# Self attention's key product by seven products of 2x2 blocks in place of eight, with both halves' scores behind the seventh product

## The chip, the cores and the metric

The kernel runs on one core of one Trainium2 chip, in one launch. The metric is device time in microseconds (us). A core has a matrix engine (TensorE, PE in the profile), a vector engine (VectorE, DVE), a scalar engine (ScalarE, ACT), GpSimd (POOL) and SyncE (SP), which here only issues DMAs. Each takes its instructions in the order written; an instruction may first wait until a semaphore has reached a count.

## The reference, cut to what matters

A decoder layer on 8 sequences of 100 tokens with 512 features, a context of 722 rows for each, and a second feed-forward part whose output is scaled by a gate. All is fp32.

```python
x0 = layernorm(x)                                   # (8, 100, 512)
q = x0 @ in_proj_w[:512].T + in_proj_b[:512]
k = x0 @ in_proj_w[512:1024].T + in_proj_b[512:1024]   # <- the product that is changed
v = x0 @ in_proj_w[1024:].T + in_proj_b[1024:]
sa = softmax(q @ k.T / sqrt(512)) @ v @ out_proj_w.T + out_proj_b
y = layernorm(x0 + sa) * g1 + be1
y = layernorm(y + cross_attention(y, ctx)) * g2 + be2
y = layernorm(y + relu(y @ w1.T + b1) @ w2.T + b2) * g3 + be3
x = x + y
out = x + gate_weight(x1 @ Wg) * (relu(x1 @ ffn_w1) @ ffn_w2)   # x1 = layernorm(x)
```

## The kernel before, in words

**Tiling.** The 800 tokens are two halves h of 400 columns (4 sequences each). Features lie on the partitions, as 4 chunks k of 128. A weight product ("unit" n, half h) of a 512x512 matrix makes 4 groups e of 128 output features, each in one PSUM bank: 4 chunks times 3 matmuls of 128x400. Three, since each fp32 operand is split into a high part (rounded to fp32r by ACT, names ending in H) and a low part (the rest, by a subtraction on DVE or POOL, ending in L): high times high, high times low, low times high. So a unit's half is 48 matmuls (lines 808 to 810).

**Self attention.** U_Q makes qT, U_K makes kT, U_VO is the output projection already multiplied by the value weights (`combine_high`, `combine_low` at the start). S_CQ and S_CK are the query and key weights of cross attention, which are multiplied together later (`combine_cross`). The order on PE (lines 1122 to 1144):

```python
unit(U_Q, 0); unit(U_K, 0, [0]); to_features(0, 1, tiles[1]); unit(U_K, 0, [1, 2, 3])
unit(U_Q, 1); self_scores(0); unit(U_K, 1); self_prob_transpose(0); combine_bias()
self_scores(1); self_attend(0); unit(U_VO, 0, [0, 1, 2]); self_prob_transpose(1)
unit(U_VO, 0, [3]); self_attend(1); to_tokens(1, 0, U_VO, XS); unit(U_VO, 1, [0, 1, 2])
```

`self_scores(h)` multiplies qT and kT of a half. DVE takes the maximum (`self_max`), ACT the exponential (`self_exp`), DVE the reciprocal (`self_normalise`), ACT scales (`self_normalise`), PE transposes (`self_prob_transpose`), ACT copies to sprobT (`self_probT`), and PE multiplies by the tokens (`self_attend`). ACT and DVE split the result into QH and QL (`self_attended`), the operand of U_VO. `self_attend(1)` writes bank k only when DVE has taken group k of U_VO's first half out of it (line 1011).

**Where splits and loads stand.** ACT splits the weights of a later unit between the groups of an earlier one (`SPLIT_AT`, line 1270): S_CQ in unit (U_K, 1), S_CK in unit (U_VO, 0), two chunks behind group 0, one behind group 1, one behind group 2. ACT's `self_probT(1)` comes behind group 2's. The low parts of S_CQ and S_CK are POOL's. DVE makes three sums of weights by a bias vector (`bias_product`: u_o, u_q, u_k); u_q reads the raw S_CQ weights in WR, u_k the raw S_CK weights in WR.

**SP's queue.** All loads are in one queue, in order: the context ct(0), the weights S_CQ, cn(0), ct(1), the weights S_CK, U_CV, and so on. ct(1) goes where ct(0) lay, so its two halves wait for DVE's `split_ct(0, 0)` and `split_ct(0, 1)` (line 558). S_CK goes to WR, so it waits for S_CQ's low parts and for u_q (lines 546 and 548). It stands behind ct(1).

**Products of 2x2 blocks.** `strassen(n)` (line 820) is already used for five feed-forward units: the 512x512 weights and the 512x800 operand are cut in 2x2 blocks, POOL makes four sums of weight blocks and four of operand blocks, ACT and DVE split them, PE makes 7 products of 12 matmuls in place of 8 (84 matmuls for both halves in place of 96), and DVE adds them up.

## Time and profile before

| what | value |
|---|---|
| time, median of 3 runs | 511.75 us (511.29 to 511.86) |
| the profiled execution's own time | 512.02 us |
| its span, first to last instruction | 510.1 us |
| PE busy | 503.7 us, 99% of the span, 2958 matmuls |
| DVE busy | 374.3 us, 73% |
| ACT busy | 242.7 us, 48% |
| POOL busy | 137.5 us, 27% |
| granted TensorE clock, mean | 1.000 |

Busy is the time in which an engine works on an instruction; waits for semaphores are not in it. PE's busy time counts pipelined matmuls, so it says that PE is never left waiting, not that each matmul takes the time shown for it: the distance from one start to the next does. The chain that ended last is followed back from the end of the program, at each step to what released the instruction.

### The profile page before, as it was taken

Reading aid. Unit: us, or ns where it says so; the run is one execution under the profiler, and the core shown is the slowest. Engines: PE = TensorE matmul, PEld = TensorE weight load, DVE = VectorE, ACT = ScalarE, POOL = GpSimd, SP = SyncE. Lnnn points to the kernel's source line nnn. Section 1 sums busy time; section 2 is a strip of 40 time slices with the busy share of each in tenths; the row PEclk is TensorE's granted clock in tenths of the full one; section 3 lists DMA queues with packets and bytes.
Section 4 is the critical chain, followed back from the end, with each engine's and each line's share of the span. In section 5 each row is a group of like instructions: output and inputs, shape, how many; then the busy total and the mean of one; then the engine's idle time right before and its main releaser. Section 6 shows DMA issues by size and latency. Waiting matters only on the chain.

```text
span 510.1 us, 7640 instructions
## 1 busy us (share of the span) xinstructions
PE 503.7 (99%) x2958; PEld 485.2 (95%) x2958; DVE 374.3 (73%) x644; ACT 242.7 (48%) x429; POOL 137.5 (27%) x104
## 2 busy tenths in 40 slices
PE   8999999999999999999999999999999999999997
PEld 6899999899988888999999999999999899999996
DVE  4853769786799896787699777368586878796645
ACT  3853652465598876164644334206536632442210
POOL 2430541014023134154504000444438313030000
PEclk9999999999999999999999999999999999999999
DMA  8951122031689961213521242002202022202004
GB/s 222 349 206 59 60 84 82 1 116 59 225 287 325 318 219 49 82 25 123 125 82 66 89 159 84 1 1 75 91 2 82 2 84 82 84 0 84 2 0 130
DMA packets 18508, 53.76 MB, mean 105 GB/s; under 512 B 1704, under 2 KB 2504, under 8 KB 15912
## 3 DMA queue, kind: packets, MB, share of 16 engines
q1 hardware_dynamic: 18412, 53.21, 31.5%
q8 instruction: 24, 0.39, 0.3%
q10 hardware_dynamic: 60, 0.07, 0.1%
q14 instruction: 12, 0.10, 0.1%
HBM read 51.63 MB, written 1.64 MB: 104 GB/s over the span
## 4 chain that ended last, share of the span: by engine, by line
PE 97%; DMA 1%; SPq 1%; DVE 0%; issue 0%; ACT 0%; DVEq 0%
PE ps L808 18%; PE ps L810 18%; PE ps L809 18%; PE ps L872 5%; PE ps L871 5%; PE ps L870 5%; PE ps L926 3%; PE ps L900 2%; PE ps L1067 2%; PE ps L1068 2%; PE ps L1069 2%; PE ps L1041 2%; PE ps L1043 2%; PE ps L1042 2%; DMA OR<-wvo_in 1%; PE ps L1013 1%
## 5 line engine op out<-in xcount | busy, mean ns | idle before, releaser
L808 PE MATMUL ps<-AH,WH 128*128 128x400 f32 x284 | 98.5, 347 | 0.0
L810 PE MATMUL ps<-AH,WL 128*128 128x400 f32 x284 | 98.0, 345 | 0.0
L809 PE MATMUL ps<-AL,WH 128*128 128x400 f32 x284 | 97.9, 345 | 0.0
L808 PE MATMUL ps<-XH,WH 128*128 128x400 f32 x192 | 66.7, 347 | 0.0
L810 PE MATMUL ps<-XH,WL 128*128 128x400 f32 x192 | 66.3, 345 | 0.0
L809 PE MATMUL ps<-XL,WH 128*128 128x400 f32 x192 | 66.2, 345 | 0.0
L651 POOL TENSOR_TENSOR WL<-WR,WH 128x512 fp32r<-128x512 f32 x29 | 41.4, 1457 | 69.8 <-ACT WH L1233 69.8
L808 PEld LDWEIGHTS ps<-AH,WH 128*128 128x128 f32 x284 | 53.4, 188 | 0.2
L809 PEld LDWEIGHTS ps<-AL,WH 128*128 128x128 f32 x284 | 53.4, 188 | 0.0
L810 PEld LDWEIGHTS ps<-AH,WL 128*128 128x128 f32 x284 | 53.4, 188 | 0.0
L1233 ACT ACTIVATE WH<-WR 128x512 fp32r<-128x512 f32 x60 | 34.1, 624 | 25.5 <-DMA WR<-wts_in 25.5
L1312 ACT ACTIVATE AH<-AT 128x400 fp32r<-128x400 f32 x40 | 21.2, 538 | 49.5 <-DVE AT L1660 32.6
L1622 DVE TENSOR_TENSOR acc<-ps,acc 128x400 f32<-128x400 f32 x47 | 26.5, 569 | 17.8 <-PE ps L810 17.6
L1579 DVE TENSOR_TENSOR ctL<-ctR,ctH 128x1444 fp32r<-128x1444 f32 x16 | 27.6, 1726 | 13.4 <-ACT ctH L1241 13.2
L808 PEld LDWEIGHTS ps<-XH,WH 128*128 128x128 f32 x192 | 36.1, 188 | 0.4 <-issue 0.2
L809 PEld LDWEIGHTS ps<-XL,WH 128*128 128x128 f32 x192 | 36.1, 188 | 0.1
L810 PEld LDWEIGHTS ps<-XH,WL 128*128 128x128 f32 x192 | 36.1, 188 | 0.0
L656 POOL TENSOR_TENSOR cnL<-cnR,cnH 128x1024 fp32r<-128x1024 f32 x7 | 16.9, 2411 | 53.4 <-ACT cnH L1247 53.4
L1665 DVE SCALAR_TENSOR_TENSOR AL<-AT,AH 128x400 fp32r<-128x400 f32 x40 | 28.1, 721 | 1.6
L1263 ACT ACTIVATE AT<-ps,cst 128x400 f32<-128x400 f32 x16 | 9.5, 595 | 40.7 <-PE ps L810 40.7
L645 POOL TENSOR_TENSOR rstd<-veps,nhalf 100x4 f32<-100x4 f32 x10 | 13.5, 1349 | 51.3 <-DVE veps L1747 51.2
L1574 DVE TENSOR_TENSOR WL<-WR,WH 128x512 fp32r<-128x512 f32 x28 | 18.2, 684 | 10.0 <-ACT WH L1233 10.0
(245 smaller groups left out, 1195.6 us busy)
## 6 DMA issues: line engine op xcount, KB each, us to landing
WR<-wts_in SPq DMA_DIRECT2D x19, 1024.0 KB, 4.8
ctR<-ctxt_in SPq DMA_DIRECT2D x16, 722.0 KB, 6.7
cnR<-ctxn_in SPq DMA_DIRECT2D x16, 512.0 KB, 4.9
cnR<-ctxn_in SPq DMA_DIRECT2D x8, 256.0 KB
tok<-x_in SPq DMA_DIRECT2D x8, 192.0 KB, 8.6
tok<-x_in SPq DMA_DIRECT2D x1, 1536.0 KB
cnR<-ctxn_in SPq DMA_DIRECT2D x8, 160.0 KB
VR<-wvo_in SPq DMA_DIRECT2D x4, 256.0 KB, 6.4
```

Source lines behind the costliest of these rows:

```text
L651: pool.tensor_tensor(WL[SLOT[n]][:, k, :], WR[:, k, :], raw(WH[SLOT[n]][:, k, :]), ALU.subtract).then_inc(w_low_pool, 1)
L808: pe.matmul(dst, wh, half(mh, h, k), start=(k == 0), stop=False)
L809: pe.matmul(dst, wh, half(ml, h, k), start=False, stop=False)
L810: mm = pe.matmul(dst, wl, half(mh, h, k), start=False, stop=(k == KC - 1))
L870: pe.matmul(dst, ah[:, k, cols], bh[:, k, :], start=(k == 0), stop=False)
L871: pe.matmul(dst, ah[:, k, cols], bl[:, k, :], start=False, stop=False)
L872: mm = pe.matmul(dst, al[:, k, cols], bh[:, k, :], start=False, stop=(k == 1))
L1233: act.activation(WH[SLOT[n]][:, k, :], raw_weights[:, k, :], ACT.Copy).then_inc(w_high, 1)
L1312: act.activation(half(AH, h, e), half(AT, h, e), ACT.Relu).then_inc(act_evac, 1)
L1579: dve.tensor_tensor(ctL[b % 2][:, 2 * i:2 * i + 2, 0:M], raw_ct(b, i), raw(ctH[b % 2][:, 2 * i:2 * i + 2, 0:M]), ALU.subtract).then_inc(ct ...
L1622: dve.tensor_tensor(half(acc, h, e), src, half(acc, h, e), ALU.add).then_inc(dve_evac, 1)
L1665: dve.scalar_tensor_tensor(out=half(AL, h, e), in0=half(AT, h, e), scalar=0.0, in1=raw(half(AH, h, e)), op0=ALU.max, op1=ALU.subtract).the ...
```

## The change

U_K is made by seven products of 2x2 blocks. The first two stand where unit (U_K, 0) stood; the other five follow unit (U_Q, 1). Both `self_scores` follow the seventh product, then `combine_bias`, then `self_prob_transpose(0)`. The raw key weights' sums are POOL's; the operand's sums t1 and t2 are DVE's, t3 and t4 POOL's. DVE adds the products up (`key_add`), in place of ACT's four evacuations for each half. ACT's splits of S_CQ, which stood in unit (U_K, 1), now stand between `self_normalise(0)` and `self_probT(0)`; DVE's `split_ct(0, 0)` and `split_ct(0, 1)` move behind u_q, whose last two steps move behind `self_normalise(1)`. cn(0)'s load waits for all of kT. The diff, cut:

```diff
-WHOLE = [n for n in LOADED if n not in STRASSEN]
+WHOLE = [n for n in LOADED if n not in STRASSEN and n != U_K]
...
             def load_cn(b, pieces=range(3)):
                 if b == 0:
-                    wait_w_low(sp, U_K, KC // 2 - 1)
-                    wait_w_low(sp, U_K, KC - 1)
+                    sp.wait_ge(k_out, 8)
...
             split_weights(U_Q, range(KC // 2))
-            for k in range(KC // 2, KC):
-                pool.wait_ge(w_high, KC * WHOLE.index(U_K) + k + 1)
-                pool.tensor_tensor(WL[SLOT[U_K]][:, k, :], WRK[:, k, :], raw(WH[SLOT[U_K]][:, k, :]),
-                                   ALU.subtract).then_inc(wk_low_pool, 1)
+            pool.wait_ge(wk_loaded, 16)
+            pool.tensor_tensor(s1, a21, a22, ALU.add).then_inc(k_sum, 1)
+            pool.wait_ge(k_sum, 1)
+            pool.tensor_tensor(s2, s1, a11, ALU.subtract).then_inc(k_sum, 1)
             inverse_deviation(1, 1)
-            pool.wait_ge(vo_made, KC)
+            pool.wait_ge(k_sum, 2)
+            pool.tensor_tensor(s4, a12, s2, ALU.subtract).then_inc(k_sum, 1)
+            pool.tensor_tensor(s3, a11, a21, ALU.subtract).then_inc(k_sum, 1)
+            pool.wait_ge(x_ready, KC)
+            for i in range(2):
+                ks = slice(2 * i, 2 * i + 2)
+                pool.tensor_tensor(X0[:, ks, :], raw(XH[0][:, ks, :]), raw(XL[0][:, ks, :]), ALU.add).then_inc(k_x0, 1)
+            pool.wait_ge(k_tsum, 2)
+            pool.wait_ge(k_x0, 2)
+            pool.tensor_tensor(t3, t2, X0[:, 0:2, :], ALU.subtract).then_inc(k_tsum_pool, 1)
+            pool.tensor_tensor(t4, t2, X0[:, 2:4, :], ALU.subtract).then_inc(k_tsum_pool, 1)
+            pool.wait_ge(s_scores, 1)
...
+            def key_products(products):
+                moving = [b(0, 0), b(0, 2)] + [key_sums(t) for t in range(4)] + [b(1, 2)]
+                for i in products:
+                    block_of = [0, 1, 3, 4, 2, 5, 6][i]
...
+                    for e in range(2):
+                        if e == 0:
+                            pe.wait_ge(k_low, block_of + 1)
+                            if 2 <= i < 6:
+                                pe.wait_ge(k_tlow, [1, 3, 4, 2][i - 2])
+                        if i < 2:
+                            pe.wait_ge(act_evac, act_count(U_Q, 0, 2 * i + e))
+                        elif i < 4:
+                            pe.wait_ge(k_tsum, 2)
+                        elif i < 6:
+                            pe.wait_ge(act_evac, act_count(U_Q, 1, 2 * (i - 4) + e))
+                        else:
+                            pe.wait_ge(k_three, e + 1)
...
             def self_scores(h):
-                pe.wait_ge(act_evac, act_count(U_K, h, KC - 1))
-                pe.wait_ge(x_ready, 2 * KC)
+                pe.wait_ge(act_evac, act_count(U_Q, h, KC - 1))
+                pe.wait_ge(k_out, 4 * (h + 1))
+                pe.wait_ge(k_two, 2)
...
             unit(U_Q, 0)
-            unit(U_K, 0, [0])
+            key_products([0])
             to_features(0, 1, tiles[1])
-            unit(U_K, 0, [1, 2, 3])
+            key_products([1])
             unit(U_Q, 1)
+            key_products(range(2, 7))
             self_scores(0)
-            unit(U_K, 1)
+            self_scores(1)
+            combine_bias()
             self_prob_transpose(0)
-            combine_bias()
-            self_scores(1)
             self_attend(0)
...
+            split_key(0)
+            split_key(1)
+            split_key(2)
             unit(U_Q, 0, [0, 1, 2])
             normalise(0, 1, tiles[1])
             unit(U_Q, 0, [3])
-            unit(U_K, 0, [0])
+            split_key(3)
+            act.wait_ge(k_sum, 4)
+            act.wait_ge(k_low, 3)
+            for e in range(2):
+                act.wait_ge(gemm_done, key_done(0, e))
+                act.activation(kmid[:, e, :], ps[:, KEY_BANKS[0] + e, 0:HALF], ACT.Copy).then_inc(k_first, 1)
             norm_features(0, 1)
-            unit(U_K, 0, [1, 2, 3])
+            for i in (4, 5, 6):
+                split_key(i)
+            split_key_sum(0)
+            unit(U_Q, 1, [0])
+            split_key_sum(3)
+            unit(U_Q, 1, [1])
+            split_key_sum(1)
+            split_key_sum(2)
+            unit(U_Q, 1, [2, 3])
+            self_exp(0)
             split_ct(0, 0)
-            unit(U_Q, 1)
-            self_exp(0)
-            split_ct(0, 1)
-            unit(U_K, 1, [0])
             self_normalise(0)
-            unit(U_K, 1, [1, 2, 3])
+            for k in range(KC):
+                split_weights(S_CQ, k)
             self_probT(0)
             self_exp(1)
             self_attended(0)
             self_normalise(1)
+            split_ct(0, 1)
             unit(U_VO, 0, [0, 1, 2])
             self_probT(1)
...
+            split_key(0)
+            split_key(1)
+            split_key(2)
             normalise(0, 1, tiles[1])
+            split_key(3)
             norm_features(0, 1)
+            dve.wait_ge(k_x0, 1)
+            dve.wait_ge(k_sum, 4)
+            dve.tensor_tensor(t1, ps[:, 4:6, 0:HALF], X0[:, 0:2, :], ALU.subtract).then_inc(k_tsum, 1)
+            dve.wait_ge(k_tsum, 1)
+            dve.tensor_tensor(t2, ps[:, 6:8, 0:HALF], t1, ALU.subtract).then_inc(k_tsum, 1)
+            for e in range(2):
+                key_add(1, e, half(kT, 0, e), kmid[:, e, :], k_out, col=e)
+            for i in (4, 5, 6):
+                split_key(i)
+            split_key_sum(0, 1); split_key_sum(3, 2); split_key_sum(1, 3); split_key_sum(2, 4)
...
-            unit(U_K, 0)
-            split_ct(0, 0)
-            unit(U_Q, 1)
-            bias_product(u_o, OR, C_BV, None, u_o_ready)
+            for e in range(2):
+                key_add(2, e, kmid[:, e, :], kmid[:, e, :], k_two)
+            for e in range(2):
+                key_add(3, e, half(kT, 1, 2 + e), kmid[:, e, :], k_three)
+            for e in range(2):
+                key_add(4, e, half(kT, 0, 2 + e), half(kT, 1, 2 + e), k_out, ALU.subtract, 2 + e)
+            bias_product(u_o, OR, C_BV, None, u_o_ready, [0, 1])
+            for e in range(2):
+                key_add(5, e, kmid[:, e, :], kmid[:, e, :], k_four)
+                key_add(5, e, half(kT, 1, 2 + e), half(kT, 1, 2 + e), k_out, col=2 + e)
+            bias_product(u_o, OR, C_BV, None, u_o_ready, [2, 3])
+            for e in range(2):
+                key_add(6, e, half(kT, 1, e), kmid[:, e, :], k_out, col=e)
+            self_max(0)
...
-            self_max(0)
             self_normalise(0)
-            split_ct(0, 1)
-            bias_product(u_q, WR, C_CBK, S_CQ, u_q_ready)
+            self_max(1)
             dve.wait_ge(vo_bias, 1)
-            self_max(1)
+            bias_product(u_q, WR, C_CBK, S_CQ, u_q_ready, [0, 1])
             self_attended(0)
             self_normalise(1)
+            bias_product(u_q, WR, C_CBK, S_CQ, u_q_ready, [2, 3])
+            split_ct(0, 0)
+            split_ct(0, 1)
             dve.wait_ge(vob_ready, 1)
             unit(U_VO, 0, [0, 1])
             bias_product(u_k, WR, C_CBQ, S_CK, u_k_ready, [0])
```

In the diff the pieces follow each other as SP, POOL, PE, ACT (from the first `split_key(0)`) and DVE (from the second). Each product of `key_products` and group e has the 6 matmuls of `strassen`. Not shown: `combine_bias` writes bank 3 instead of 7, and new tiles and semaphores.

## Rows read from the trace of the kernel before

**Rows 1.** The page, its chain that ended last, by engine.

```profile
PE 97%; DMA 1%; SPq 1%; DVE 0%; issue 0%; ACT 0%; DVEq 0%
```

**Rows 2.** Waits of PE over the whole span: total us, times, longest us.

```profile
PE ps L945 <- ACT OH L1424: 1.3, 1, 1.3
PE ps L926 <- DVE acc L2087: 0.2, 1, 0.2
```

**Rows 3.** Timeline of PE: start us, us, engine, line, output and inputs, count.

```profile
1.73 4.73 PE L1117 MATMUL ps<-ident 128*128 128x128 f32 x22 [1.73 <-POOL ones L641]
...
20.51 0.34 PE L808 MATMUL ps<-XH,WH 128*128 128x400 f32 x1
...
31.28 0.34 PE L810 MATMUL ps<-XH,WL 128*128 128x400 f32 x1
...
48.41 2.99 PE L937 MATMUL ps<-kT,qT 128*100 128x100 f32 x32
...
60.37 0.97 PE L967 MATMUL ps<-ones,u_o 128*128 128x1 f32 x8
61.20 3.05 PE L937 MATMUL ps<-kT,qT 128*100 128x100 f32 x32
64.09 3.74 PE L1013 MATMUL ps<-sprobT,tok 100*128 100x100 f32 x32
67.61 0.42 PE L808 MATMUL ps<-QH,WH 128*128 128x400 f32 x1
...
76.80 3.71 PE L1013 MATMUL ps<-sprobT,tok 100*128 100x100 f32 x32
...
82.01 0.43 PE L808 MATMUL ps<-QH,WH 128*128 128x400 f32 x1
```

**Rows 4.** Timeline of ACT in the same stretch.

```profile
52.25 0.34 ACT L1368 ACTIVATE sprob<-ps,snb 100x100 f32<-100x100 f32 x1 [3.04 <-DVE snb L1801]
...
53.54 1.42 ACT L1241 ACTIVATE ctH<-ctR 128x1444 fp32r<-128x1444 f32 x1
54.84 0.60 ACT L1257 ACTIVATE kT<-ps,cst 128x400 f32<-128x400 f32 x1
...
56.35 1.19 ACT L1376 ACTIVATE sprob<-sprob,srec 100x100 f32<-100x100 f32 x4
...
70.18 2.18 ACT L1233 ACTIVATE WH<-WR 128x512 fp32r<-128x512 f32 x4
74.79 0.51 ACT L1381 ACTIVATE sprobT<-ps 100x400 f32<-100x400 f32 x1 [2.43 <-PE ps L1002]
```

**Rows 5.** Timeline of DVE in the same stretch.

```profile
43.86 2.33 DVE L1722 SCALAR_TENSOR_TENSOR u_o<-OR,cst,u_o 128x512 f32<-128x512 f32 x3
...
51.43 0.57 DVE L1799 TENSOR_REDUCE smx<-ps 100x4 f32<-100x400 f32 x1 [4.98 <-PE ps L937]
...
54.99 1.67 DVE L1579 TENSOR_TENSOR ctL<-ctR,ctH 128x1444 fp32r<-128x1444 f32 x1 [1.12 <-ACT ctH L1241]
...
58.13 5.03 DVE L1722 SCALAR_TENSOR_TENSOR u_q<-WR,cst,u_q 128x512 f32<-128x512 f32 x3
...
66.93 2.04 DVE L1811 TENSOR_TENSOR QL<-ps,QH 128x400 fp32r<-128x400 f32 x4 [1.87 <-ACT QH L1387]
...
74.15 1.51 DVE L1720 TENSOR_SCALAR u_k<-WR,cst 128x512 f32<-128x512 f32 x1
...
77.17 0.74 DVE L1722 SCALAR_TENSOR_TENSOR u_k<-WR,cst,u_k 128x512 f32<-128x512 f32 x1
```

**Rows 6.** Timeline of SP's DMA queue: the issue of S_CK's weights.

```profile
63.23 0.35 SPq L551 DMA_DIRECT2D WR<-wts_in  x1
```

**Rows 7.** DMA issues between 60 and 70 us: KB, us from issue to landing.

```profile
WR<-wts_in SPq DMA_DIRECT2D x1, 1024.0 KB, 4.8
```

**Rows 8.** Timeline of POOL: the low parts of S_CK's four chunks.

```profile
70.88 5.94 POOL L651 TENSOR_TENSOR WL<-WR,WH 128x512 fp32r<-128x512 f32 x4 [8.27 <-ACT WH L1233]
```

**Rows 9.** Groups by line and form, of the five units made by blocks: busy us, mean ns.

```profile
L704 POOL TENSOR_TENSOR TS<-XF,TS 128x800 f32<-128x800 f32 x2 | 4.2, 2080 | 0.2
...
L1631 DVE TENSOR_TENSOR TL<-TS,TH 128x800 fp32r<-128x800 f32 x8 | 7.8, 984 | 0.7 <-ACT TH L1278 0.6
```

More of the change, by code:

```diff
@@ L41 @@
 LOADED = [n for n in range(NU) if n not in (U_VO, U_A)]
-KINDS = (["fp32", "fp32", "residual", None, None, "split", "residual"]
+KINDS = (["fp32", "key", "residual", None, None, "split", "residual"]
          + ["relu_bias", "down_residual"] + ["relu_bias", "down_add"] * (NF - 1)
@@ L117, in dve_writes @@
 def dve_writes(n):
-    return KINDS[n] not in ("fp32", "down_first")
+    return KINDS[n] not in ("fp32", "key", "down_first")
 def groups(n, h):
-    if n not in STRASSEN:
+    if n not in STRASSEN and n != U_K:
         return KC
-    first = 2 if n == PARTED else 5
+    first = 2 if n in (PARTED, U_K) else 5
     return 2 * first if h == 0 else PRODUCTS - 2 * first
@@ L419, in wait_w_low @@
                 before -= 1
-            if n == U_K and k >= KC // 2:
-                eng.wait_ge(wk_low_pool, k - KC // 2 + 1)
-                return
-            if n not in (U_Q, U_K):
+            if here and n != U_Q:
                 before -= KC // 2
@@ L1214, in split_weights @@
             def split_weights(n, k):
-                raw_weights = WRK if n == U_K else WR
                 if n == U_Q and k == 0:
@@ L1255, in unit @@
                     if kind == "fp32":
-                        dst, col = (qT, C_BQ) if n == U_Q else (kT, C_BK)
-                        act.activation(half(dst, h, e), src, ACT.Identity,
-                                       bias=cst[:, col + e:col + e + 1]).then_inc(act_evac, 1)
+                        act.activation(half(qT, h, e), src, ACT.Identity,
+                                       bias=cst[:, C_BQ + e:C_BQ + e + 1]).then_inc(act_evac, 1)
                     elif kind == "split":
@@ L1439, in _, with split_key, split_key_sum @@
                            ACT.Copy).then_inc(small_high, 1)
-            for k in range(KC):
-                split_weights(U_K, k)
+            def split_key(i):
+                hi, _, src = key_block(i)
+                if i < 3:
+                    act.wait_ge(wk_loaded, 16)
+                    src = raw_key_block([0, 1, 1][i], [0, 0, 1][i])
+                else:
+                    act.wait_ge(k_sum, {3: 3, 4: 4, 5: 1, 6: 3}[i])
+                act.activation(hi, src, ACT.Copy).then_inc(k_high, 1)
+            def split_key_sum(t):
+                if t in (0, 3):
+                    act.wait_ge(k_tsum, 1 if t == 3 else 2)
+                else:
+                    act.wait_ge(k_tsum_pool, t)
+                hi, _, whole = key_sums(t)
+                act.activation(hi, whole, ACT.Copy).then_inc(k_thigh, 1)
+            split_key(0)
+            split_key(1)
+            split_key(2)
             unit(U_Q, 0, [0, 1, 2])
```

97 lines of the change are left out of this document (85 added, 12 removed).

## The prediction

> **What bounds the kernel now.** I read the chain that ended last first: 97% of it is PE [rows 1]. Then PE's waits over the whole span: 1.3 us before its work on the weights at the start, 0.2 us at the end, and nothing between [rows 2]. So from 14 to 506 us PE never stops, and the change is worth what it takes from PE's own work, less every wait it brings in. A wait here is not hidden by anything. The other engines idle a good part of the time, so I need their queues only for the points at which PE asks them for something. For these I read the four timelines from 20 to 92 us side by side [rows 3 to 5], [rows 8].
>
> **What it removes on PE.** 96 matmuls become 84. Sixty of them run from 20.51 to 31.28 us [rows 3], 59 steps in 10.77 us or 0.1825 us each (the 0.34 us shown are pipelined). 12 x 0.1825 = 2.19 us. That is the whole of the possible gain, 0.4%.
>
> **The products themselves.** The first five blocks' sums are ready long before use, so I only follow the operand's sums. DVE's t1 and t2 can start when the second half's features are split (about 35.3 us: PE's transposes of them end near 33.0 as before, and ACT first copies the first product), and take some 0.98 us each [rows 9]: 37.2. POOL's t3 and t4 take 2.1 each [rows 9]: 41.4. Behind them ACT's and DVE's split of t4, about 1.9 us, if in series: 43.3, and DVE's queue, which holds three block splits and four sum splits, ends at about 44.8. PE comes out of unit (U_Q, 1) at 33.0 + 60 x 0.1825 = 43.9 and needs t2 first, then t3 at 46.1 and t4 at 48.3. Covered by 1.5 us or more; I put these at nothing, and up to 1 us if POOL and DVE hold each other up. The last key sums follow the seventh product: DVE has two bias steps of u_o at 0.75 [rows 5] and two additions behind it, ready about 57.3, while PE starts the second scores at 57.8. Nothing again, but with only 0.5 us to spare.
>
> **The first new wait: scores to sprobT.** Before, the softmax of half 0 had unit (U_K, 1) as its cover; now only the second scores and the bias columns cover it. The first scores stood at 48.41 [rows 3], behind 96 matmuls of U_Q and 48 of U_K; now 96 and 84 stand in front of them, 36 more: 48.41 + 36 x 0.1825 = 54.98. Two times scores at 64.09 - 61.20 = 2.89 and the bias columns at 61.20 - 60.37 = 0.83 [rows 3] later PE is free: 61.6. ACT's side: from the start of the scores to the end of the exponentials 53.54 - 48.41 = 5.13 us [rows 3, 4], split_ct(0, 0) 54.84 - 53.54 = 1.30 to the next start, scaling 1.19 [rows 4]: 62.6. PE waits 1.0 us. Behind the scaling ACT now has the four S_CQ splits, 2.18, and sprobT, 0.51 [rows 4], less about 0.2 for overlapping ends: 65.1. Without waits `self_attend(0)` would start 0.35 us (four small transposes) behind 61.6; it starts at 65.1, so the second wait is 2.15 us and both are 3.15. From its start to U_VO it is 67.61 - 64.09 = 3.52 [rows 3]: U_VO starts at 68.6, 1.0 us later than before. The gain is already gone.
>
> **The second new wait: S_CK's weights.** This is the large term. ACT's four S_CK splits stand in unit (U_VO, 0) in front of `self_probT(1)`, as before. Before, SP had issued the load at 63.23 [rows 6] and it landed 4.8 us later [rows 7], two us before ACT came to it at 70.18 [rows 4]. Now it is late, by this queue:
> - `self_attended(0)` ends on DVE 4.88 us behind the start of `self_attend(0)` (66.93 + 2.04 - 64.09) [rows 3, 5]: 70.0, and the reciprocal at 70.1.
> - Only then come u_q's last two steps, 2 x 0.75 [rows 5]: 71.6. POOL is done with S_CQ by then.
> - Then split_ct(0, 0) and split_ct(0, 1), 1.67 each [rows 5]: 73.2 and 74.8. ACT has its half of the second ready at 72.7, in time.
> - SP sends ct(1)'s halves at 73.2 and 74.8 and S_CK at about 75.2. Alone it lands after 4.8 us [rows 7]: 80.0. It shares the engines with ct(1)'s second half, 0.7 MB in front of its 1.0 MB, so up to 2 us more. I take 81.0.
> - ACT's four splits, 2.18 less overlap, then sprobT 0.51 [rows 4]: 83.7.
>
> PE would have come to `self_attend(1)` at 68.6 + (76.80 - 67.61) = 77.8 [rows 3]. It starts at 83.7: 5.9 us of waiting.
>
> **The third: DVE behind the same load.** Group 3 of `self_attend(1)` needs U_VO's group 3 out of its bank. In DVE's queue that is behind two steps of u_k, which need S_CK. The first starts at 81.7; it and the evacuation of group 2 take 77.17 - 74.15 = 3.02 us [rows 5]. In that stretch POOL was splitting S_CK's low parts (70.88 to 76.82) [rows 8]; now POOL starts at the same moment as DVE and goes on to about 88, so the next two are slow too: u_k's step about 1.68 (u_q's three took 5.03 beside POOL, u_o's three 2.33 alone) [rows 5], the evacuation about 1.5. End 87.9. PE, at some 0.9 us a group (3.71 for four) [rows 3], has done three by 86.4 and waits 1.5 us. From the start of `self_attend(1)` to U_VO's second half it was 82.01 - 76.80 = 5.21 [rows 3]; now 83.7 + 5.21 + 1.5 = 90.4, against 82.0.
>
> By the Trainium skill ("GPSIMD Engine Reference", section 1, Specifications) GpSimd shares its SBUF interfaces with VectorE, in contention with instructions that have two SBUF inputs. The rows on u_q and u_o agree. By it the evacuation's first instruction, whose tensor comes from PSUM, keeps its speed, and its second and u_k's step lose theirs, as I have it. Did nothing lose any, DVE would be there before PE, and the sum would be 1.5 us less.
>
> **Sum.** 90.4 - 82.0 = +8.4 us: -2.19 of matmuls and waits of 1.0, 2.15, 5.9 and 1.5. Behind this point the order is the old one, everything of S_CK is done when `combine_cross` asks for it, and PE had no slack to make good: the 8.4 us reach the end. The profiled execution took 512.02 us with its span of 510.1 inside it, so 520.4 by its own measure; the median of the runs lies 0.3 lower: 520.2.
>
> **Bounds.** Landing between 80.0 and 83.0 us: -1 to +2. Contention: -1.5 to +0.5. ACT's chain at the first scores: 0.5 either way. Operand sums late: 0 to +1. Together about 517.5 to 523.
>
> **Rivals.**
> - *The clock falls in the long wait.* From rest PE is slow: the 22 warm-up matmuls of 128 columns took 0.215 us each (4.73 / 22), the 32 of the scores, of the same type and 100 columns, 0.093 (2.99 / 32), or 0.12 for 128 columns [rows 3]. That is the ratio of 1.2 GHz to 2.4, though the granted clock is given as 1.00 for the whole span. After 5.9 us without work PE may be there again. A slow piece as long as the warm-up loses 2.4 us; the first 1.5 of them fall in the wait for group 3 and cost nothing. That gives 520.2 to 522.6, at best guess 521.3. No wait of before is long enough to show it. 25 in 100. The Trainium skill ("TensorE: Matmul & The Clock Gate", Part 1) has the clock halve for an idle engine and come back with activity; by it this case is more likely than not, at 521.3.
> - *The load is in time.* Were S_CK not late (an order on DVE or SP other than I read, so that it is issued before about 72 us), only the softmax waits remain: 511.75 - 2.19 + 3.15 = 512.7. Against it: two splits of ct and u_q's last steps are ahead of it in DVE's own order. 5 in 100.
> - *Faster.* ACT gets to sprobT of half 0 before PE asks, and the load is in time too. The first needs 3.15 us off a chain whose every member has a row. It gives 509.6, and decides from the point at which `self_attend(0)` follows the transposes without a gap. 3 in 100.
> - *Worse.* The load lands at 83 or later, since ct(1) fills the queues, and DVE and POOL slow each other throughout: 523 to 525. 9 in 100.
> - My forecast as summed: 58 in 100, with its own range 518.8 to 522.
>
> A measurement of this kernel tells 0.2% (1 us) from no change. Faster by more: 0.03; the same: 0.02; slower: 0.95. The range 517.8 to 523.5 leaves out the load in time, the faster case and most of the worse one.
>
> **What would show it.** In the profile after: 12 matmuls fewer; first scores near 55.0; a PE wait on ACT's sprob of about 1 us, one on sprobT of about 2, and one on the second sprobT of about 6 us near 78 to 84; ACT waiting for the DMA of WR for about 8 us from 72.7; SP's issue of S_CK near 75; a wait of `self_attend(1)` on DVE of 1 to 2 us; none behind it. If ACT does not wait for WR, the prediction falls. If PE waits before the first scores, the operand sums are what I got wrong.

## The result and the profile after

The changed kernel takes 537.92 us, median of 6 runs (536.86 to 540.0), and the kernel before, run beside it, 511.89 us (511.29 to 512.26, 6 runs): ratio 1.0511, 95% interval 1.0496 to 1.0527. So it is slower by 26 us, where 8.4 were forecast and 523.5 us was the top of the range. The profiled execution took 538.64 us, its span is 536.6 us.

The page after: busy time by engine, the granted clock of TensorE in 40 slices of 13.4 us each, and the chain that ended last.

```profile
PE 515.1 (96%) x2946; PEld 496.4 (93%) x2946; DVE 397.3 (74%) x669; ACT 244.0 (45%) x430; POOL 148.2 (28%) x110
...
PEclk9978978599999999999999999999999999999999
...
PE 88%; DVE 4%; DMA 3%; ACT 2%; POOL 1%; issue 1%; SPq 1%; DVEq 0%
```

2958 matmuls became 2946, and yet PE was busy for 11.4 us longer (515.1 against 503.7). The clock row shows why: five of its first eight slices are below 9 (7, 8, 7, 8, 5), where the kernel before had 1.000 on the mean. PE's share of the chain fell from 97% [rows 1] to 88%. These are two different losses, and the next views take them apart. First PE's waits: total us, times, longest.

```profile
PE ps L1099 <- ACT sprobT L1463: 7.9, 2, 6.0
PE ps L983 <- ACT tok L1418: 6.1, 1, 6.1
...
PE ps L1086 <- ACT sprob L1458: 1.0, 1, 1.0
```

Before, nothing of the kind stood there [rows 2]. The new waits are 15.0 us. Now PE's timeline. The wait in front of a group is in brackets.

```profile
37.71 2.93 PE L983 MATMUL ps<-ident,tok 100*128 100x100 f32 x16 [6.09 <-ACT tok L1418]
...
64.03 5.81 PE L1021 MATMUL ps<-kT,qT 128*100 128x100 f32 x64
...
71.69 0.55 PE L1086 MATMUL ps<-ident,sprob 100*100 100x100 f32 x4 [1.03 <-ACT sprob L1458]
74.15 6.59 PE L1099 MATMUL ps<-sprobT,tok 100*128 100x100 f32 x32 [1.91 <-ACT sprobT L1463]
80.45 0.68 PE L860 MATMUL ps<-QH,WH 128*128 128x400 f32 x1
...
97.87 7.15 PE L1099 MATMUL ps<-sprobT,tok 100*128 100x100 f32 x32 [5.99 <-ACT sprobT L1463]
...
108.09 0.68 PE L860 MATMUL ps<-QH,WH 128*128 128x400 f32 x1
```

`self_attend(0)` is the same 32 matmuls as in [rows 3] and takes 6.59 us where it took 3.74; the first matmul of U_VO's half takes 0.68 where it took 0.42 [rows 3]. The windows give the clock beside it. Columns: stretch, its length, then busy us and count of PE, PEld, DVE, ACT and POOL, and behind them PE's granted clock.

```profile
34.00:44.00 10.00, 6.29 (x27) 6.26 (x28) 7.81 (x11) 6.70 (x14) 2.20 (x3) 0.50 0.00 0
44.00:56.00 12.00, 12.00 (x68) 12.00 (x66) 9.87 (x12) 5.37 (x8) 4.13 (x2) 1.00 0.01 3
...
74.00:76.00 2.00, 1.85 (x11) 1.85 (x12) 1.46 (x1) 1.74 (x10) 2.00 (x2) 0.70 0.00 0
76.00:84.00 8.00, 8.00 (x34) 7.97 (x34) 4.37 (x8) 3.66 (x9) 1.82 (x2) 0.50 0.00 0
84.00:86.00 2.00, 2.00 (x10) 1.99 (x9) 2.00 (x2) 0.50 (x1) 0.00 (x0) 0.74 0.00 0
86.00:95.00 9.00, 5.88 (x35) 5.49 (x33) 2.79 (x5) 0.00 (x0) 0.00 (x0) 1.00 0.79 281
95.00:109.00 14.00, 11.13 (x51) 11.05 (x52) 10.85 (x14) 4.59 (x9) 5.91 (x4) 0.51 0.21 76
```

Three stretches run at 0.50, which is the lower of the two levels (1.2 in place of 2.4 GHz). The first begins at 33.8, 2.2 us into the wait on `tok`; the second at 74.8, 0.65 us after the end of the wait on sprobT; the third at 95.3, 3.4 us into the second wait on sprobT. Each ends while PE works without a gap. What a stretch costs is PE's busy time in it times what is missing of the clock: 6.29 x 0.50 = 3.15; 1.85 x 0.30 + 8.00 x 0.50 + 2.00 x 0.26 = 5.1; 11.13 x 0.49 = 5.45. Together 13.7 us. This is an estimate, and PE's busy time bears it out: 13.7 less the 2.19 us of the 12 matmuls is 11.5, and PE was busy for 11.4 us longer.

**The sum.** -2.19 (12 matmuls fewer) + 15.0 (waits) + 13.7 (clock) = 26.5 us. The spans differ by 536.6 - 510.1 = 26.5. Nothing is left over behind 109 us.

**The wait that was not foreseen** is the first. PE's transposes of the second half's tokens wait for ACT's normalisation, and ACT for DVE's `nmr`, a product of 100x4 numbers. DVE's and POOL's timelines around it:

```profile
29.98 6.13 DVE L1867 SCALAR_TENSOR_TENSOR nmr<-mv,rstd 100x4 f32<-100x4 f32 x1 [0.92 <-POOL rstd L678]
36.02 0.99 DVE L1872 TENSOR_SCALAR tok<-tok,mv,rstd 100x512 f32<-100x512 f32 x2
...
27.34 2.60 POOL L678 TENSOR_TENSOR rstd<-veps,nhalf 100x4 f32<-100x4 f32 x1 [0.81 <-DVE veps L1860]
29.92 1.29 POOL L755 TENSOR_TENSOR KXS<-WRK,WS 128x512 f32<-128x512 f32 x1
31.17 1.26 POOL L756 TENSOR_TENSOR KXS<-WRK 128x512 f32<-128x512 f32 x1
32.40 3.68 POOL L760 TENSOR_TENSOR X<-XH,XL 128x800 f32<-128x800 f32 x2
```

The record of `nmr` begins at 29.98 and ends at 36.11. In the kernel before and in e1 below, without the four POOL instructions beside it, it takes 0.16 us. They are s4, s3 and the two halves of X0, they run back to back from 29.92 to 36.08, and `nmr` is done 0.03 us later.

**The wait that was foreseen**, on S_CK. SP's queue, and ACT behind it:

```profile
85.01 1.96 SPq L593 DMA_DIRECT2D ctR<-ctxt_in  x2
87.06 17.10 SPq L585 DMA_DIRECT2D WR<-wts_in  x2
...
95.24 2.19 ACT L1316 ACTIVATE WH<-WR 128x512 fp32r<-128x512 f32 x4 [10.74 <-DMA WR<-wts_in]
97.34 0.48 ACT L1463 ACTIVATE sprobT<-ps 100x400 f32<-100x400 f32 x1
```

S_CK is issued at 87.06, right behind both halves of ct(1), and ACT can begin at 95.24, 8.2 us later. Alone it took 4.8 [rows 7].

### The profile page after: what moved, and what is told of

Same layout as the page of the kernel before. It is cut to its first block, busy times and chain, and to the rows that moved or that the text cites. A ratio compares the mean times of both kernels' runs of the same rounds, so it can differ in the third digit from the quotient of the medians.

```text
span 536.6 us, 7662 instructions
## 1 busy us (share of the span) xinstructions
PE 515.1 (96%) x2946; PEld 496.4 (93%) x2946; DVE 397.3 (74%) x669; ACT 244.0 (45%) x430; POOL 148.2 (28%) x110
## 4 chain that ended last, share of the span: by engine, by line
PE 88%; DVE 4%; DMA 3%; ACT 2%; POOL 1%; issue 1%; SPq 1%; DVEq 0%
PE ps L860 15%; PE ps L861 15%; PE ps L862 15%; PE ps L924 5%; PE ps L923 5%; PE ps L922 5%; PE ps L1009 3%; PE ps L1099 3%; PE ps L983 2%; PE ps L1153 2%; PE ps L1154 2%; PE ps L1155 2%; PE ps L1127 2%; PE ps L1129 2%; PE ps L1128 2%; DMA WR<-wts_in 2%
## 5 line engine op out<-in xcount | busy, mean ns | idle before, releaser
L860 PE MATMUL ps<-XH,WH 128*128 128x400 f32 x160 | 55.6, 347 | 0.0
L862 PE MATMUL ps<-XH,WL 128*128 128x400 f32 x160 | 55.2, 345 | 0.0
L861 PE MATMUL ps<-XL,WH 128*128 128x400 f32 x160 | 55.2, 345 | 0.0
L1316 ACT ACTIVATE WH<-WR 128x512 fp32r<-128x512 f32 x60 | 33.8, 623 | 36.4 <-DMA WR<-wts_in 36.4
L860 PEld LDWEIGHTS ps<-XH,WH 128*128 128x128 f32 x160 | 30.1, 188 | 0.4 <-issue 0.2
L861 PEld LDWEIGHTS ps<-XL,WH 128*128 128x128 f32 x160 | 30.1, 188 | 0.1
L862 PEld LDWEIGHTS ps<-XH,WL 128*128 128x128 f32 x160 | 30.1, 188 | 0.0
L678 POOL TENSOR_TENSOR rstd<-veps,nhalf 100x4 f32<-100x4 f32 x10 | 14.7, 1469 | 53.7 <-DVE veps L1860 53.7
L1687 DVE TENSOR_TENSOR WL<-WR,WH 128x512 fp32r<-128x512 f32 x28 | 18.3, 685 | 10.3 <-ACT WH L1316 10.3
```

Source lines behind the costliest of these rows:

```text
L860: pe.matmul(dst, wh, half(mh, h, k), start=(k == 0), stop=False)
L861: pe.matmul(dst, wh, half(ml, h, k), start=False, stop=False)
L862: mm = pe.matmul(dst, wl, half(mh, h, k), start=False, stop=(k == KC - 1))
L1316: act.activation(WH[SLOT[n]][:, k, :], WR[:, k, :], ACT.Copy).then_inc(w_high, 1)
```

## The experiments

Each ratio is to runs of the kernel before beside it on the same chip (medians 511.47 to 511.86 us); not all experiments ran on one chip. Waits and clocks are those of one profiled execution of each kernel. "After" is the changed kernel.

### Is it POOL's work beside nmr?

**e1_pool_waits** is after, with POOL's s4, s3 and X0 behind the normalised tokens:

```diff
             inverse_deviation(1, 1)
+            pool.wait_ge(tok_ready, B)
             pool.wait_ge(k_sum, 2)
             pool.tensor_tensor(s4, a12, s2, ALU.subtract).then_inc(k_sum, 1)
```

> The changed kernel, but POOL waits until the second half's tokens are normalised (tok_ready at 8) before it makes s4, s3 and X0. Theory: the 4-element nmr instruction on DVE took 6.13 us only because POOL's four tensor instructions ran beside it; then it takes 0.2 us here, the first PE wait of 6.1 us goes, the clock does not fall before 74 us, and 6.1 + 3.2 us come back less 1 to 2 us, since the key sums and the features of half 1 now start later: 529 to 531 us. Rival: nmr is late for a reason of its own (its operands, the pow on POOL); then it stays near 6 us and the time is 538 or more.

Measured: 531.49 us (530.53 to 532.39), ratio 1.0383 (1.0351 to 1.0415), 6.4 us under after. PE's waits:

```profile
PE ps L1100 <- ACT sprobT L1464: 8.7, 2, 6.8
...
PE ps L1087 <- ACT sprob L1459: 1.0, 1, 1.0
PE ps L861 <- DVE XL L1889: 0.8, 1, 0.8
PE ps L954 <- issue: 0.7, 1, 0.7
```

The wait on `tok` is gone. Two small ones have come for it, on XL and for the third product, and the second wait on sprobT is 0.8 us longer. The clock still falls three times, at 66.5, 87.0 and 110.9 us. The last fall is new: it is 3.4 us long with PE busy throughout, which costs 1.7 us. With these the time sits just above the range expected, and the sum closes here too: -2.19 + 11.2 of waits + 11.6 of clock = 20.6, and the spans differ by 530.5 - 510.1 = 20.4.

**e5_before_pool3** and **e6_before_pool1** go the other way: the kernel before, with three or one additions of 128x800 given to POOL behind the same `inverse_deviation(1, 1)`. Nothing uses the results; POOL's next work and DVE's `split_ct(0, 0)` wait until they are written.

```diff
             inverse_deviation(1, 1)
+            pool.wait_ge(x_ready, KC)
+            for i in range(3):       # e6: range(1)
+                pool.tensor_tensor(extra[i][:, :, :], raw(XH[0][:, 0:2, :]), raw(XL[0][:, 0:2, :]), ALU.add).then_inc(extra_done, 1)
+            pool.wait_ge(extra_done, 3)  # e6: 1
             pool.wait_ge(vo_made, KC)
...
             unit(U_K, 0)                 # DVE
+            dve.wait_ge(extra_done, 3)   # e6: 1
             split_ct(0, 0)
```

> The kernel before, with three POOL additions of 128x800 (1.9 us each, results unused) right behind the pow that gives rstd of half 1. Nothing else is changed. Theory: DVE's nmr instruction (4 elements) doesn't get through while POOL runs one after the other; it takes 5.5 to 6 us instead of 0.16, PE waits as long in front of the transposes, and after some 5.7 us of idling the clock falls to half and costs about 3 us more: 520 to 521 us. Rival: beside POOL a DVE instruction takes about twice its time, as u_q did; then nmr takes 0.3 us and the time is 512.

> The same with one such addition. Theory: nmr lasts as long as that one, 1.9 us; PE waits 1.7 us, too short for the clock to fall: 513.5 us. Rival as for three: 512.

Measured: e5 519.44 us (518.83 to 520.58), ratio 1.0151 (1.0132 to 1.0169); e6 514.86 us (513.22 to 515.67), ratio 1.0054 (1.0033 to 1.0076). DVE's and POOL's timelines, of e5:

```profile
29.52 5.52 DVE L1760 SCALAR_TENSOR_TENSOR nmr<-mv,rstd 100x4 f32<-100x4 f32 x1 [0.91 <-POOL rstd L647]
...
29.45 5.56 POOL L723 TENSOR_TENSOR extra<-XH,XL 128x800 f32<-128x800 f32 x3
```

and of e6:

```profile
29.49 1.87 DVE L1760 SCALAR_TENSOR_TENSOR nmr<-mv,rstd 100x4 f32<-100x4 f32 x1 [0.91 <-POOL rstd L647]
...
29.43 1.92 POOL L723 TENSOR_TENSOR extra<-XH,XL 128x800 f32<-128x800 f32 x1
```

`nmr` ends 0.03 us after POOL in e5 (35.04 against 35.01) and 0.01 after it in e6, as in after. PE waits 5.2 and 1.7 us, and the clock is at 0.50 from 35.2 to 42.0 and from 34.0 to 37.4. The window of e6:

```profile
33.96:37.36 3.40, 3.40 (x15) 3.38 (x14) 2.12 (x5) 1.59 (x4) 0.00 (x0) 0.50 0.09 21
```

e5 is 0.6 us below the range expected. e6 was expected at 513.5, with a wait too short for a fall, and missed by 1.4 us: the clock fell. Three of its four runs took 514.76 to 515.67 us with a mean clock of 0.995 to 0.997; the fourth took 513.22 with 1.000. So POOL's work at this place makes the wait on its own, in a kernel that has nothing else of the change, and the length of the wait follows POOL's. By the Trainium skill ("SBUF — State Buffer", section "SBUF: two separate sides") GpSimd and a VectorE instruction with two SBUF inputs take one shared pair of ports in turn, whoever starts first for its whole instruction. The rows agree that `nmr` stands still; they show more than that, since it stood through up to four POOL instructions in a row. No run here changes only what `nmr` reads, so that it is the ports that hold it is not shown; that POOL's work holds it is.

### Is the rest the clock?

**e2_fill** is after, with 24 matmuls of 128x400 in the first wait, in front of the transposes. They write banks that later products start anew, and leave nothing out.

```diff
             key_products([0])
+            pe.wait_ge(vo_low, KC)
+            for i in range(24):
+                pe.matmul(ps[:, 4 + i // 6, 0:HALF], WH[SLOT[U_Q]][:, 0, 0:P], half(XH, 0, 0), start=True, stop=True)
             to_features(0, 1, tiles[1])
```

> The changed kernel with 24 extra matmuls of 128x400 (4.4 us, results overwritten) in the first wait of PE, between the first product and the transposes of the second half. The wait for the tokens keeps its end at 37.7 us. Theory: the half-rate clock from 33.8 to 44.1 us is caused by the idle PE; it stays at 1.00 there, and the 6.3 us of work in it take 3.15: 534.8 us. Rival: the clock falls for another reason or costs nothing: 538 us. The later two falls stay.

Measured: 535.4 us (534.26 to 536.94), ratio 1.0462 (1.0428 to 1.0495), 2.5 us under after. The window that had 0.50 in after:

```profile
34.00:44.00 10.00, 8.55 (x56) 8.21 (x55) 7.81 (x12) 7.29 (x15) 2.20 (x2) 1.00 0.01 2
```

The wait on `tok` is 1.4 us now, the rest of it is filled, and the clock stays at 1.00. `nmr` is held as before (6.22 us), so here the data come no earlier; only the clock is other, and 2.5 of its 3.15 us come back. The two later falls stay. The time alone would be weak evidence, since the interval of the ratio reaches 1.7 us either way; the granted clock shows it.

### Is it the load's place in the queues, or its lateness?

**e3_sck_behind** takes S_CK out from in front of the second sprobT:

```diff
-            unit(U_VO, 0, [0, 1, 2])      # ACT, S_CK's splits between its groups
             self_probT(1)
-            unit(U_VO, 0, [3])
             self_attended(1)
+            unit(U_VO, 0)
             normalise(1, 0, tiles[0])
...
-            (DVE: u_k's four steps between U_VO's groups)
             self_attended(1)
+            bias_product(u_k, WR, C_CBQ, S_CK, u_k_ready)
```

> The changed kernel, but ACT's splits of S_CK and DVE's three u_k steps stand behind self_attended(1), so that neither sprobT of half 1 nor U_VO's evacuation waits for the load. Theory: the PE wait of 6.0 us goes and with it the third fall of the clock (11.1 us of work at half rate, 5.5 us): 538 - 11.5 = 526.5 us, within 1 us. Rival by the prediction's own sum (a wait without a clock): only 6.0 to 7.5 us, 530.5 to 532. Rival: something else holds self_attend(1) as late: no change.

Measured: 536.26 us (535.52 to 537.62), ratio 1.0477 (1.044 to 1.0515). That is 10 us over what was expected, and its interval overlaps that of after. The second wait on sprobT is gone, but PE waits 5.34 us further on for `tok` of the next normalisation. DVE's timeline:

```profile
95.94 1.62 DVE L1832 TENSOR_SCALAR u_k<-WR,cst 128x512 f32<-128x512 f32 x1
97.60 5.06 DVE L1834 SCALAR_TENSOR_TENSOR u_k<-WR,cst,u_k 128x512 f32<-128x512 f32 x3
102.58 2.48 DVE L1852 BATCH_NORM_STATS2 bnst<-ps 100x6 f32<-100x512 f32 x4
...
106.81 0.16 DVE L1866 SCALAR_TENSOR_TENSOR nmr<-mv,rstd 100x4 f32<-100x4 f32 x1
```

u_k needs S_CK and now stands ahead of the statistics. It comes as late as the load, takes 6.7 us since POOL splits S_CK's low parts beside it, and hands the wait on. So it is the lateness of the load that costs. Moving its users moves the wait.

**e4_scq_early** moves ACT's four S_CQ splits from in front of sprobT(0) to in front of `self_exp(0)`:

```diff
             unit(U_Q, 1, [2, 3])
+            for k in range(KC):
+                split_weights(S_CQ, k)
             self_exp(0)
             split_ct(0, 0)
             self_normalise(0)
-            for k in range(KC):
-                split_weights(S_CQ, k)
```

> The changed kernel, but ACT splits S_CQ before self_exp(0), in its idle stretch from 54 to 67 us. Theory: the wait for the first sprobT falls from 1.9 us to about nothing. With 1.0 us of wait left the clock may stay up: then 10.2 us of work at half rate (5.1 us) come back too: 538 - 7 = 531 us. If the clock falls all the same, 536 us. S_CK's load is as late relative to its use, or more so, since PE comes to it earlier: up to 5 us of the gain may be lost there, so 531 to 536 and the split of it in the trace decides.

Measured: 536.48 us (534.71 to 538.5), ratio 1.0482 (1.0442 to 1.0522), which can't be told from after. The first sprobT wait falls from 1.9 to 0.5 us, the one on sprob grows from 1.0 to 1.7. The clock falls at this place all the same, from 72.6 to 82.9, as the expectation had it for 536 us.

**e8_loads_early** is the full repair of the second half alone: e4's edit, and u_q ahead of everything that depends on `self_attended(0)`, and S_CK ahead of ct(1) in SP's queue.

```diff
-            load_ct(1)                                   # SP
             load_weights(S_CK)
+            load_ct(1)
...
+            split_weights(S_CQ)                          # POOL
             pool.wait_ge(s_scores, 1)
...
-            split_weights(S_CQ)
...
             self_max(0)                                  # DVE
+            bias_product(u_q, WR, C_CBK, S_CQ, u_q_ready, [0, 1])
...
-            bias_product(u_q, WR, C_CBK, S_CQ, u_q_ready, [0, 1])
+            bias_product(u_q, WR, C_CBK, S_CQ, u_q_ready, [2, 3])
             self_attended(0)
             self_normalise(1)
-            bias_product(u_q, WR, C_CBK, S_CQ, u_q_ready, [2, 3])
```

ACT's `split_ct(0, 0)` moves behind its `self_normalise(1)` too. **e7_both** is e8 and e1 together, and DVE's queue of the first half in the order of need:

```diff
             split_key(0)
+            normalise(0, 1, tiles[1])
             split_key(1)
             split_key(2)
-            normalise(0, 1, tiles[1])
...
-            for i in (4, 5, 6):
-                split_key(i)
+            split_key(4)
             split_key_sum(0, 1)
+            split_key(5)
+            split_key(6)
```

> The changed kernel with only the second repair. Theory: the first wait (6.1 us) and the first fall of the clock (3.2 us) stay, everything behind is gone: 510.1 + 9.3 = 519.4, between 518.5 and 520.5. Rival: the second half's waits come back in another place (S_CK still late): 525 or more.

> The changed kernel repaired in both places. First: POOL waits for the second half's tokens before s4, s3 and X0; DVE normalises them before it splits key blocks 1 and 2; t2's low part stands before those of blocks 5 and 6. Second: S_CQ's splits in ACT's idle stretch, its low parts and u_q at once, S_CK's load in front of ct(1)'s, the splits of ct(0) behind self_normalise(1). Theory (waits and the clock they bring down are the whole loss): no wait over 0.7 us is left, the clock stays up, and the 12 matmuls show: 511.7 - 2.2 + 0.6 = 510.1, between 509.6 and 511.2. Rival (the seven products carry a cost of their own): 512 or more with the waits gone.

Measured: e8 525.95 us (524.49 to 527.31), ratio 1.0275 (1.0247 to 1.0302); e7 519.66 us (517.83 to 520.66), ratio 1.0154 (1.0134 to 1.0174). With after (1.0511) and e1 (1.0383) this is a table of two by two: POOL's place is worth 1.3% with the loads late and 1.2% with them in time (DVE's order with it), the loads 2.3 to 2.4%, and 1.5% stays with both repairs. PE's waits in e8, where the 6.0 us on the second sprobT are gone:

```profile
PE ps L983 <- ACT tok L1418: 5.8, 1, 5.8
PE ps L1099 <- DVE XS L1728: 2.1, 2, 1.8
...
PE ps L1099 <- ACT sprobT L1463: 0.6, 1, 0.6
```

The 2.1 us on XS stand where the prediction had its third wait (1.5 us), but they are not that wait: the load is in time here (issued at 71.50), and 1.8 of the 2.1 are for group 2, not group 3. DVE is late because its two ct splits, which wait for ACT's halves, stand from 78.64 to 81.88 right in front of U_VO's groups, and POOL splits S_CK's low parts beside it from 80.50 on.

e8 and e7 missed their times by 6.5 and 9.6 us: e8 has the XS wait and a fall of the clock that begins in it (87.3 to 94.1), which I had left out. e7 has 1.8 us on XS too, and the profiled run is the fastest of its five (517.83 us, mean clock 0.993, the others 0.990 to 0.992). In e7, PE's timeline

```profile
47.42 0.42 PE L954 MATMUL ps<-TH,KXH 128*128 128x400 f32 x1 [1.41 <-issue]
...
64.34 5.66 PE L1100 MATMUL ps<-sprobT,tok 100*128 100x100 f32 x32 [0.59 <-ACT sprobT L1464]
```

and its windows

```profile
56.00:66.00 10.00, 9.15 (x94) 8.80 (x92) 7.89 (x18) 4.82 (x22) 0.14 (x2) 1.00 0.46 148
66.00:72.00 6.00, 6.00 (x27) 5.98 (x26) 2.38 (x5) 2.27 (x7) 0.00 (x0) 0.50 0.51 177
```

show a fall at 66.0 with no wait near it longer than 0.6 us, in the run of scores, bias columns, transposes and `self_attend(0)`. The 1.41 us in front of the fourth product is a split of an operand's sum (a TL) that DVE makes beside POOL's low parts of S_CQ, which e8's edit had moved there.

### Is it the run of small matmuls?

**e10_scores_between** is e7 with half 0's scores between the sixth and the seventh product, so that no two scores follow one another (and DVE's `self_max(0)` ahead of the last `key_add`). **e11_before_scores_last** puts the order of the change alone into the kernel before: 96 matmuls for U_K, and both halves' scores behind them, with ACT's and DVE's queues to match.

```diff
-            key_products(range(2, 7))       # e10
+            key_products(range(2, 6))
             self_scores(0)
+            key_products([6])
+            combine_bias()
             self_scores(1)
-            combine_bias()
...
-            self_scores(0)                  # e11
             unit(U_K, 1)
-            self_prob_transpose(0)
-            combine_bias()
+            self_scores(0)
             self_scores(1)
+            combine_bias()
+            self_prob_transpose(0)
             self_attend(0)
```

> e7_both with one change of order: half 0's scores in front of the seventh product, the bias columns behind it, half 1's scores last. Theory: in e7_both the clock fell at 66 us with no wait above 0.6 us near, because both halves' scores, the bias columns, the transposes and self_attend(0) stand in one run of small matmuls; with the seventh product between them it does not fall: 3.3 us less than e7_both, so 515 to 516.5 us by the median of the runs. Rival (the short waits there alone bring it down): as e7_both, 519.7.

> The kernel before, all 96 matmuls of U_K kept, but in the order of the change behind them: unit (U_K, 1), then both halves' scores, the bias columns, the transposes, self_attend(0). The splits of the weights stay where they are and ct(0) is not in the softmax's way. Theory: half 0's softmax has 3.7 us of cover for 4.5 us of work, and the run of small matmuls brings the clock down for some 7 us: 1.4 us of waits and 3.3 us of clock: 515 to 516.5 us. Rival: only the waits count: 512.5 to 513.

Measured: e10 518.44 us (517.63 to 520.34), ratio 1.0139 (1.0121 to 1.0158), 2 us over what was expected; e11 512.95 us (512.51 to 517.67, 10 runs), ratio 1.0053 (1.0028 to 1.0078). In e10 the clock does not fall at 66 us, but it is at 0.50 from 82.0 to 88.8, behind and between waits on XS of 2.5 us in all:

```profile
82.00:88.80 6.80, 6.40 (x30) 6.08 (x30) 5.17 (x10) 1.01 (x2) 0.00 (x0) 0.50 0.43 149
```

The runs of e10 and e7 overlap (517.63 to 520.34 and 517.83 to 520.66), so only the one profile of each shows that difference. By the median e11 is what its rival had, waits alone (512.5 to 513), and not the 515 to 516.5 expected. But six of ten runs took 512.5 to 513.0 us with a mean clock of 1.000 or 0.999, and four took 515.8 to 517.7 with 0.990 to 0.993; the profiled run is one of the six. So the order of the change costs about 1 us by its own wait (0.6 on sprobT) and in some executions 3 to 5 us more at a lower mean clock. That two halves' scores with nothing between them make the fall likelier agrees with e7, e10 and e11, but it is not shown: e11's profiled run has them next to one another and no fall, and no run singled out what in that stretch brings one.

### What is the change worth without its waits?

**e9_tuned** is e10 with four pieces of work moved to where their engine has room:

```diff
+            pool.wait_ge(k_tlow, 4)                      # POOL
             split_weights(S_CQ)
...
+            act.wait_ge(gemm_done, key_done(5, 1))       # ACT
+            split_ct(0, 0)
+            split_ct(0, 1)
             self_exp(0)
...
-            bias_product(u_q, WR, C_CBK, S_CQ, u_q_ready, [0, 1])   # DVE, in front of qk
...
             self_normalise(0)
+            bias_product(u_q, WR, C_CBK, S_CQ, u_q_ready)
             dve.wait_ge(vo_bias, 1)
...
+            self_max(1)
             self_attended(0)
```

**e12_tuned2** is e9 with its last two waits taken away:

```diff
-            self_scores(1)
+            self_scores(1, [0, 1, 2])
             self_prob_transpose(0)
+            self_scores(1, [3])
             self_attend(0)
...
-            unit(U_VO, 0, [2])
-            bias_product(u_k, WR, C_CBQ, S_CK, u_k_ready, [1])
-            unit(U_VO, 0, [3])
-            bias_product(u_k, WR, C_CBQ, S_CK, u_k_ready, [2, 3])
+            unit(U_VO, 0, [2, 3])
+            bias_product(u_k, WR, C_CBQ, S_CK, u_k_ready, [1, 2, 3])
```

> The kernel repaired in both places, and further: half 0's scores stand between the sixth and the seventh product, the bias columns in front of half 1's scores; POOL leaves S_CQ until DVE has split the operand's sums; ACT splits ct(0) while PE is at the seventh product; all of u_q stands in front of half 1's maximum. Theory: waits are the 0.6 us for sprobT and little else, the clock stays at 1.00 since dense products cut the run of small matmuls in two: 511.5 - 2.2 + 0.9 = 510.2, between 509.4 and 511.3, so faster than before by 0.2%. Rival: the clock falls all the same: 513.5.

> The tuned order again (e9_tuned: 513.06 us), with its two last waits taken away. The four transposes of half 0's probabilities stand in front of the last sequence's scores of half 1, so that 8 matmuls of scores (0.7 us) cover ACT's copy to sprobT; that wait of 0.6 us should be gone. DVE takes group 3 of U_VO's first half out of its bank before the second step of u_k, not behind it, so self_attend(1) should not wait (0.7 us on XS and 0.25 us of slower groups). Together 1.2 to 1.5 us: 511.7 us, no more than the kernel before, and the second half of U_VO starts 1.2 us or more earlier than in it (82.01) if PE's first product starts at the same time. Rival: what the tuned order lost is not in these waits but in short falls of the clock that come in some executions only; then the median stays at 512.7 or more though the waits are gone. A second rival: the steps of u_k that now stand behind group 3 hold up DVE's QL of half 1, and PE waits for it in front of U_VO's second half by up to 0.7 us.

Measured: e9 513.06 us (512.45 to 514.34, 7 runs), ratio 1.0025 (1.001 to 1.004); e12 512.06 us (511.17 to 514.21, 12 runs), ratio 1.0006 (0.9992 to 1.0019). Neither profile has a fall of the clock before the last microseconds. e9 was expected at 509.4 to 511.3 us, faster than before; it took 513.06 and is slower by 0.25%, so that expectation failed too. e12 came 0.4 us over its 511.7. PE's waits in e9:

```profile
PE ps L1101 <- DVE XS L1732: 0.7, 1, 0.7
PE ps L1101 <- ACT sprobT L1466: 0.6, 1, 0.6
...
PE ps L955 <- issue: 0.3, 1, 0.3
```

and in e12:

```profile
PE ps L985 <- ACT tok L1423: 0.4, 1, 0.4
PE ps L955 <- issue: 0.3, 1, 0.3
```

In e12 U_VO's second half starts at 80.83 us, 1.18 earlier than in before [rows 3]. Of this 0.69 us are left at the next normalised tokens' transposes (87.97 against 88.66), behind the new wait of 0.4 us for them, 0.40 at the transposes behind (105.03 against 105.43), and as much at the end of the span (509.7 against 510.1). What takes the part between 88 and 105 us is not shown. So the best version ties with the kernel before, and the 2.19 us of fewer matmuls buy nothing that can be measured. Neither rival of e12 holds: the median went down with the waits, and PE does not wait for QL.

## Why the prediction was wrong

It had the sign (95 in 100 for slower), all three waits at the softmax and at S_CK, and their causes. The time was off by 17.7 us. Its sum was 8.4 us and the measured one is 26.5. Two terms that stood at nothing make the difference, a wait of 6.1 us before the first scores and 13.7 us of clock, less the 1.5 of the third wait, which did not come (18.3 us, where the sums differ by 18.1). The prediction's own steps beside what was measured, us from the start of the span:

| point | predicted | measured | later by | the new part |
|---|---|---|---|---|
| first scores | 54.98 | 64.03 | 9.05 | wait of 6.09, clock 3.15 |
| `self_attend(0)` starts | 65.1 | 74.15 | 9.05 | none |
| U_VO's first half | 68.6 | 80.45 | 11.85 | 2.8: 6.30 us for 3.52, half clock |
| S_CK issued | 75.2 | 87.06 | 11.86 | none |
| S_CK landed | 81.0 | 95.2 | 14.2 | 2.4: 8.2 us behind its issue, not 5.8 |
| PE asks for sprobT(1) | 77.8 | 91.9 | 14.1 | 2.3: U_VO at half clock up to 85 |
| `self_attend(1)` starts | 83.7 | 97.87 | 14.2 | none |
| U_VO's second half | 90.4 | 108.09 | 17.7 | 3.5: 10.22 us for 6.71, half clock |

- **The step that failed: "ready long before use, so I only follow the operand's sums", with "PE's transposes of them end near 33.0 as before".** I asked of POOL's work on the blocks' sums only whether it would be ready in time, not what it does to the engine beside it. The bound for POOL and DVE holding each other up was 1 us, and it was for t3 and t4. s4, s3 and X0 were priced at nothing; they hold a DVE instruction of 0.16 us for 6.13, and PE waits for it. e1 takes the wait away, e5 and e6 make it in the kernel before. The last line of the prediction's test, "if PE waits before the first scores, the operand sums are what I got wrong", pointed at the right stretch and the wrong sums: it is X0 and the weights' s3 and s4, not t1 to t4.
- **The clock stood at nothing in the sum, and this is the larger of the two errors.** It was a rival with 25 in 100, one fall with 1.1 us net as its best guess; it was three falls of 13.7 us. The error in the size has a plain cause: I took the warm-up's 4.73 us as the length of a slow piece. In after they are 10.3, 10.2 and 13.6 us long, from 33.8, 74.8 and 95.3, with 6.3 to 11.1 us of work in them. And I looked only behind the longest wait. The one before `self_attend(0)` (1.0 and 1.9 us) brought a fall as well. e2 shows that the first fall comes from the gap: filled, it stays away. For the second and third fall no run filled the gap; that they come from theirs is argued from their place.
- **Right: the first new wait**, 1.0 predicted and 1.03 measured, and 2.15 against 1.91 for sprobT. `self_attend(0)` is exactly as much too late as the first scores are, so ACT's chain was followed rightly. The 0.2 us by which 9.05 is less than 6.09 + 3.15 are not followed up.
- **Right in its size by two errors that cancel: the second wait**, 5.9 against 5.99. The load landed 2.4 us later than I took it, 0.4 beyond my later bound (83.0 is 7.8 us behind its issue), and PE came 2.3 us later since it was slow. The queue on DVE that delays the load was right: the issue is late by no more than what stands in front of it.
- **The third wait, 1.5 us on XS,** was not there in after, since PE came to it at half its clock and so later. DVE has group 3 out of its bank at 102.29:

```profile
101.44 0.85 DVE L1728 TENSOR_TENSOR XS<-XS,XL 128x400 f32<-128x400 f32 x1
```

  PE started at 97.87 and took 1.79 us a group (7.15 / 4), so it was there at 103.2. At the 0.93 us a group of before (3.71 / 4) [rows 3] it would have been there at 100.7 and waited 1.6 us, by this estimate.
- **The gain, 2.19 us**, is there in full as the term of the sum: the sum closes to 0.1 us.

My expectations missed too. In e7 and e8 I took the clock as settled once the long waits were gone: I expected 510.1 us of e7 and it took 519.66, and e9 missed in the same way. In e3 I followed ACT's queue past the late load and not DVE's.

## What to carry to other kernels

When work is added to an idle engine, look at what its neighbours do in those microseconds, not only at when the work is done: a small instruction on the path of the bound engine that runs beside it may be held for as long as it lasts. Where one engine carries 97% of the chain, a new wait costs more than its length, since the clock may halve in it or behind it; here 15.0 us of waits cost another 13.7. A gain of 0.4% on such an engine has to be paid for in full by cover: here the orders of PE, ACT, DVE, POOL and SP all had to be changed to get back to the time before.
